# Two edits to a fused attention and MLP kernel: shared weight tensors moved by 288 bytes in SBUF, and the next block's weights split at an earlier chunk

## What is computed

```python
def reference(x, w_qkv, w_out, W1, B1, W2, B2, LN_G, LN_B):
    xn = _layernorm(x, axis=-1)
    s = attention(xn, w_qkv, w_out)
    y = xn
    for i in range(6):
        h = gelu(einsum('bsd,hd->bsh', y, W1[i]) + B1[i])
        y = einsum('bsh,dh->bsd', h, W2[i]) + B2[i] + y
        if i < 5:
            y = layernorm(y, LN_G[i], LN_B[i])
    return x + s * silu(y)
```

## Time and profile before

| | |
|---|---|
| Median of the three runs | 1671.97 us |
| The profiled execution: its own time | 1672.36 us |
| The profiled execution: its span | 1670.7 us |
| PE busy | 1617.1 us (97%) |
| DVE busy | 1169.8 us (70%) |
| ACT busy | 856.2 us (51%) |
| POOL busy | 317.8 us (19%) |

### The profile page before, as it was taken

One profiled execution on the slowest core, in us unless ns is written; L12 is line 12 of the kernel. 1 busy time (PEld: TensorE's weight loads), 2 busy tenths in 40 slices (PEclk: granted clock), 3 DMA queues, 4 the chain that ended last, 5 costly groups with the idle time before them and its releaser, 6 DMA issues. The chain is left out here.

```text
span 1670.7 us, 28636 instructions
## 1 busy us (share of the span) xinstructions
PE 1617.1 (97%) x11024; PEld 1314.5 (79%) x11024; DVE 1169.8 (70%) x2932; ACT 856.2 (51%) x1164; POOL 317.8 (19%) x305
## 2 busy tenths in 40 slices
PE   6989999999999999999999999999999899999998
PEld 5879988889888888888888888888989844444443
DVE  7826777777777777777777677776565568787753
ACT  3444444444443444444444444444444499798986
POOL 1021111111111111111111111111011123343333
PEclk9989999999999999999999999999999989999999
DMA  8868724536002002012030020022020135565341
GB/s 276 320 173 209 174 62 109 116 73 140 15 7 61 8 16 49 7 34 42 7 51 8 23 51 9 14 39 80 1 71 1 45 114 163 162 187 178 117 116 58
DMA packets 76017, 141.46 MB, mean 85 GB/s; under 512 B 10172, under 2 KB 52924, under 8 KB 68540
## 3 DMA queue, kind: packets, MB, share of 16 engines
q1 hardware_dynamic: 75880, 139.62, 32.0%
HBM read 109.44 MB, written 55.31 MB: 99 GB/s over the span
## 5 line engine op out<-in xcount | busy, mean ns | idle before, releaser
L646 ACT ACTIVATE m_hid<-m_h_ps,m_b1s 128x512 f32<-128x512 f32 x384 | 265.3, 691 | 694.1 <-PE m_h_ps L749 674.6
L712 DVE TENSOR_TENSOR m_hidl<-m_hid,m_hidh 128x512 fp32r<-128x512 f32 x384 | 283.1, 737 | 266.5 <-ACT m_hidh L649 265.6
L993 ACT ACTIVATE a_prob<-a_st_ps 128x1024 f32<-128x1024 f32 x288 | 277.6, 1023 | 40.4 <-PE a_st_ps L1079 36.9
L762 PE MATMUL m_y_ps<-shared,m_hidh 128*128 128x256 f32 x1536 | 283.1, 282 | 0.0
L749 PE MATMUL m_h_ps<-m_xth,shared 128*128 128x512 f32 x768 | 275.7, 400 | 6.3 <-issue 3.9
L613 POOL TENSOR_TENSOR xres<-xres,m_b2s 128x1024 f32<-128x1024 f32 x48 | 132.1, 2753 | 744.1 <-DVE xres L665 744.1
L649 ACT ACTIVATE m_hidh<-m_h_ps,m_b1s 128x512 fp32r<-128x512 f32 x384 | 261.7, 682 | 0.0
L762 PEld LDWEIGHTS m_y_ps<-shared,m_hidh 128*128 128x128 f32 x1536 | 246.8, 188 | 14.5
L762 PE MATMUL m_y_ps<-w2h,m_hidh 128*128 128x256 f32 x768 | 216.9, 282 | 0.0
L762 PE MATMUL m_y_ps<-shared,m_hidl 128*128 128x256 f32 x768 | 215.3, 280 | 0.0
L762 PE MATMUL m_y_ps<-w2l,m_hidh 128*128 128x256 f32 x768 | 214.2, 279 | 0.0
(11 more groups left out here) (121 smaller groups left out, 2656.6 us busy)
## 6 DMA issues: line engine op xcount, KB each, us to landing
shared<-k_stacks SPq DMA_DIRECT2D x14, 896.0 KB
shared<-q_stacks SPq DMA_DIRECT2D x14, 896.0 KB
q_stacks<-q_parts SPq DMA_DIRECT2D x96, 128.0 KB
k_stacks<-k_parts SPq DMA_DIRECT2D x96, 128.0 KB
q_parts<-mq SPq DMA_DIRECT2D x16, 512.0 KB, 4.3
k_parts<-mk SPq DMA_DIRECT2D x16, 512.0 KB, 3.8
mk<-k_stacks SPq DMA_DIRECT2D x20, 384.0 KB, 10.7
raw<-w1t SPq DMA_DIRECT2D x48, 128.0 KB, 2.3
```

The costliest lines, as they stand in the source:

```text
L646: nc.scalar.activation(hid[n % 2][:], h_ps[n % 2][:], ACT.Gelu, bias=b1s[i % 2][:, k:k + 1])
L712: nc.vector.tensor_tensor(hidl[n % 4][:], hid[n % 2][:], hidh[n % 4][:].bitcast(F32), ALU.subtract).then_inc(low_done, 1)
L762: m = nc.tensor.matmul(y_ps[:, j, :], h[n % 4][:, j * P:(j + 1) * P], w[par][:, k, :], start=(k == 0 and j % 2 == 0 and h is hidh and w is ...
L993: nc.scalar.activation(to, scores, ACT.Exp).then_inc(exp_done, 1)
```

## The change

Two tensors, `mhalf` and the first buffer of `x_mx`, are now created ahead of `apart`. The split of the next block's piece moves from chunk 7 of a slot to chunk 4, with its wait for the raw piece. Nothing else is different.

```diff
 class MaxSearch:
-    def __init__(s, nc, b, scratch, keep):
+    def __init__(s, nc, b, scratch, keep, mx):
...
-        s.mx = [b.sb(f"x_mx{u}", [P, 2, HG, QT]) for u in range(2)]
+        s.mx = [*mx, b.sb("x_mx1", [P, 2, HG, QT])]
...
                 if t:
                     epilogue(t - 1, k)
-                if k == 7 and t < LAST:
+                if k == 4 and t < LAST:
                     dve.wait_ge(raw_loaded[g % 2], 32 * (t // 2 + 1))
                     split_piece(nc, dve, keep, (i + 1) % 2, g, w_high, t + 1).then_inc(w_split, 1)
                 for v in AT.get(n, ()):
...
         b = Bufs(nc, ctx)
+        mhalf = b.sb("mhalf", [P, TILES])
+        mx = [b.sb("x_mx0", [P, 2, HG, QT])]
         apart = [b.sb(f"apart{u}", [P, PAIR * SEQ], F32R) for u in range(2)]
         shared = [b.sb(f"shared{n}", [P, HALVES * HID], F32R) for n in range(4)]
         keep = {
-            "ident": b.sb("ident", [P, P]), "mhalf": b.sb("mhalf", [P, TILES]), "causal": b.sb("causal", [P, BANK]),
+            "ident": b.sb("ident", [P, P]), "mhalf": mhalf, "causal": b.sb("causal", [P, BANK]),
...
-        search = MaxSearch(nc, b, scratch, keep)
+        search = MaxSearch(nc, b, scratch, keep, mx)
```

## The result

The changed kernel takes 1662.67 us (median of four runs, 1661.62 to 1664.01) against 1672.84 for the kernel before beside it (median of four). The ratio is 0.9936, with a 95% interval of 0.9917 to 0.9955. The profiled execution took 1662.96 us, with a span of 1661.2.

What follows compares the result with a forecast made beforehand. TensorE, busy 97% of the span, was taken as the bound, with slower even blocks and border waits. From 1672.36 us: - 9.0 - 10.4 - 1.0 + 7.7 + 2.7 + 0.1 = 1662.5; range 1656.5 to about 1672.

Steps and rivals of the forecast that it cites:

- The shift: MLP matmuls L762 and L749: even blocks reach odd blocks' pace through low address bits, 3.0 us a block, 9.0 gained.
- The borders: Five MLP block borders: `up` no longer waits for the last split piece of the next block's weights, 10.4 us gained.
- The 1.0 us for the lower clock: Block 4: the stretch at the lower clock after its border idle goes too, 1.0 us gained (0 to 1.5).
- The first piece: Slot 0: the earlier split waits for raw piece 0, PE stands 7.7 us, plus 2.7 for the clock; 10.4 lost.
- The loss to the clock: After PE's idle in slot 0: a stretch at half clock, 2.7 us lost (0 to 5.3).
- The later pieces: Weight pieces after piece 0: SP's loads still arrive in time, slot 0's delay covering pieces 1 and 2; cost 0.
- The split on VectorE: Chunk 4, before the search visit: the 1.2 us split just fits into the idle there, 0.1 us lost in all.
- The port: Rival, chance 0.07: in chunk 4 L260 waits up to 0.68 us for POOL's `m_rstd`; 21 x 0.65 = 13.7 us, time 1676.2.
- The inert shift: Rival, chance 0.18: moving the shared tensors gains nothing, border and first piece cancel; time 1671.5, no change.
- the worse offset: Rival, chance 0.05: shared weights at the new offset lose 9.0 us and attention's L1099 2.3; time 1682.8.
- More than forecast: Rival, chance 0.04: attention gains 2.3 us and the clock does not drop in slot 0; time 1657.5.

Runs made afterwards that it cites:

- the run without the delay: Changed kernel, but slot 0 alone keeps its split in the eighth chunk (chunk 7): 1655.67 us, ratio 0.9890 to the kernel before.
- the first run: Kernel before with only the two small tensors moved to the front, the split staying in chunk 7: 1667.00 us, ratio 0.9956.
- 800: Kernel before with 800 unused bytes ahead of `apart` and 224 ahead of `w1h1`, so all later tensors move by 1024: 1664.29 us.
- 352: Kernel before with 352 unused bytes ahead of `apart` and 160 ahead of `w1h1`, so all later tensors move by 512: 1676.53 us.

## Why the prediction was right

The time, 1662.67 us, is 0.2 us from the forecast. The mechanisms were the ones forecast, but such closeness is luck: several terms were off by about a microsecond, to either side. The windows of the two profiled executions give the change by stage: 0.6 us more ahead of the MLP, 5.1 more in block 0, then 2.2, 4.6, 2.5 and 6.3 less in blocks 1 to 4, nothing in block 5, and 0.3 more in attention (339.5 and 339.8 us), together 9.5 less (span 1670.7 to 1661.2). Here are the terms one by one.

**The shift** was put at 9.0 us. Alone it gave 7.4, with an interval of 5.4 to 9.5. By blocks that run has 3.1 us less in block 0 (201.07 to 197.93), 2.6 less in block 4, and in block 2 0.8 less, or 2.5 without its stretch at the lower clock: 8.2 in all. In the changed kernel L762 fell by 2.01 us in block 2 and L749 by 1.20, 3.2 a block where 3.0 was forecast, but block 2 gained only 2.4 beside its border. Part of the difference is in the search: counted start to start, L203 takes 16.8 us of block 2 instead of 16.3. It is 16.6 in the run with the shift alone and 16.3 in the one with the split alone, so it comes with the shift. Its waits for VectorE in the MLP grew as well, from 10.3 us to 11.0; whether the search's own moved operands have a share was not tried. The reason given, the low address bits, was half of the matter: the prediction's sentence that the shared tensors "start at the same offset within 16 KiB as the second set" named the condition that came true, but the run with all tensors moved shows that the offset by itself does nothing. TensorE's pace hangs on how its two operands lie to each other, by up to (120.8 - 116.5)/116.5 = 3.7% in L762. The rule of the Trainium skill (SBUF — State Buffer, section SBUF: two separate sides), that PE never waits on anyone, by which this term would have been 0, does not agree with that. Whether the two readings of TensorE meet each other, or others' traffic, was not tried.

**The borders** (10.4) came true: no "issue" wait of 2 us is left. Block 1, whose weights' place did not change, went from 205.37 to 203.20, 2.2 us for its one border. The 1.0 us for the lower clock was right in kind and too small: block 4 gained 6.3 us where block 2 gained 4.6, and the difference is the 1.7 us that the stretch at 0.50 cost in the kernel before. The changed kernel has no such stretch behind a border.

**The first piece** (7.7 + 2.7): the idle was 7.7 us by PE's modelled ends and 8.1 by its weight loads. The raw piece was there 0.8 us later than in the earlier trace rows (127.33 for 126.52); the MLP itself had started 0.6 later. The loss to the clock was over-sized: PE worked 3.82 us at half speed in the window shown, a loss of half of that, 1.9, where 2.7 came from the 5.3 us of the earlier trace rows. Even so the whole came out as forecast: the 5.1 us of block 0, with the 2.1 of its border and the 3.1 of the shift, make 10.3. The rest is in part the start of the MLP, which ran 6.2 us at the lower clock instead of 5.3, and that is luck. In the run with the split alone all of slot 0 cost 8.8: PE was idle for 7.4 us and then worked 3.1 at half speed, a loss of 1.5. There the change gave 3.5 us, not the 0.9 that the terms make without the shift; the clock after the wait (1.5 for 2.7) and at the border (1.7 for 1.0) are the largest known parts of it.

**The later pieces** were costed at 0 because "slot 0's delay covers them". That held, and the run without the delay shows what the cover was worth: 2.2 us of PE.

**The split on VectorE** (0.1): the idle before `low` fell from 1.38 to 0.16 us and the next search matmul waits for nothing; in the run with the split alone the search's waits for VectorE in the MLP are 9.9 us, not more than before (10.3).

**The port** rival is refuted: in both kernels L260 takes 424 to 428 ns, and in the changed one it runs beside L616 in 39 slots. Its price was also a little too high: with 0.06 us of cover a wait of 0.68 leaves 0.62 a slot, not 0.65. But the two engines do meet. POOL's L616, in the kernel before and in the changed kernel:

```profile
L616 POOL TENSOR_TENSOR m_rstd<-m_var,mhalf x40: 1018/1019/1021, 138.1 to 1145.6; 128x4 f32<-128x4 f32 x40
```

```profile
L616 POOL TENSOR_TENSOR m_rstd<-m_var,mhalf x40: 1017/1191/1195, 148.2 to 1135.6; 128x4 f32<-128x4 f32 x40
```

The median (the middle figure) rose by 0.17 us; only two chunks later is the result needed. Slot 11 above is not such a case, its L616 took 1.02. Slot 10 is one:

```profile
372.71 0.29 DVE L257 CAST shared<-raw 128x256 fp32r<-128x256 f32 x1
372.88 1.19 POOL L616 TENSOR_TENSOR m_rstd<-m_var,mhalf 128x4 f32<-128x4 f32 x1 [7.33 <-DVE m_var L689]
372.91 0.28 DVE L258 CAST shared<-raw 128x256 fp32r<-128x256 f32 x1
373.23 0.43 DVE L260 TENSOR_TENSOR shared<-raw,shared 128x256 fp32r<-128x256 f32 x1
```

Of the 39 that run beside a split, 32 take 1.19 us, and in these the second cast, L258, takes its usual 0.28 to 0.29. In the other 7 L616 takes 1.02 and L258 0.31. So it seems to be the cast that L616 meets: one of the two loses time each time, 0.17 or 0.02 us, while L260 is beside all 39 and always as long. The rule of the Trainium skill on two SBUF inputs beside a GpSimd read (SBUF — State Buffer, section Who interferes with whom), which the rival took, is thus not borne out for L260 and L616: L260 does not wait, and L616 keeps its 1.02 us beside it in seven slots. The trace does agree for the longer L613: in the kernel before, each `low` that began beside one, that of the earlier trace rows among them, ended 0.55 us after L613's end, 44 times.

**The inert shift** is refuted by the first run, **the worse offset** for this change by the same, though its mechanism exists. **More than forecast** did not come either: attention did not gain, and the clock did fall in slot 0.

## What to carry to other kernels

Where the same loop goes at two speeds, compare the places of its operands in memory: here the weights' start less the partner's, modulo 256 bytes, was worth up to 3.7% of a matmul, and some filler bytes set it, so it is worth a sweep of eight values, in steps of 32 bytes. When a step is moved earlier, walk its inputs back to the queue that fetches them at the very first pass, not in the steady state; there a single late load took back as much as five removed waits gave, and issuing that load before two bulk copies gave it back. And leave a mover room on the engine it moves to by measuring the idle time before the next consumer there, as the 1.38 us were measured here.

## What the runs showed that was not expected

The pace of TensorE depends on the distance of its operands' addresses in a jagged way with a period of 256 bytes (116.5 ns at 192, 118.0 to 120.8 at all other distances seen, for matmuls of 256 columns), and moving all tensors together changes nothing. An idle of 2.1 us at a border is followed by 3.4 us at the lower clock at some borders and not at others of the same kernel: at one of five in the kernel before, at two of five in the run with the shift alone, and at one, three, two and two of five in the next four runs (288 bytes ahead of all, 288 ahead of `shared2`, 800, 352). A four-element instruction on POOL was 0.17 us longer beside the split's second cast on VectorE, or the cast was 0.02 us longer, never both; the subtraction with two SBUF inputs that runs beside it as well kept its length.
